# Histogram windows of a two-layer GNN in parts of 32 destinations, one exponential per attention tile, digits added by TensorE

## Chip, cores and metric

The kernel runs on one core of one Trainium2 chip. The metric is the device time of one execution in microseconds. Before the change the median of three runs was 514.59 us (514.49 to 516.25).

## What is computed

The input is a graph of 1250 nodes with 128 features and 20000 edges, sorted by destination. A first layer is a graph attention layer followed by a GRU cell, a second one is four steps of typed message passing, each followed by a GRU cell. Cut to the part that matters here:

```python
dst = minimum((1250 * uniform(20000) ** 2.0).astype(int32), 39999)   # then sorted, src with it
e = leaky_relu(s_s[src] + s_d[dst] + a_b[0], 0.2)
m = segment_max(e, dst)
ex = exp(e - m[dst])
attn = ex / segment_sum(ex, dst)[dst]
h_prime = segment_sum(attn[:, None] * Wh[src], dst) + h @ res_W.T + res_b
x = x + gru(h_prime, h)                       # layer 1
etypes = argmax(edge_feat, axis=1)
msg = (einsum('nd,tod->tno', h, W_edge) + b_edge[:, None, :])[etypes, src]
h = gru(segment_sum(msg, dst), h)             # layer 2, four times
```

## The kernel before

The kernel never gathers along edges. It first builds a table of counts: how many edges of each of four types run from a source to a destination. An edge type is worth 1, 16, 256 or 4096, so that the four counts of a cell are the four hexadecimal digits of one number below 65536. Sources stand on the 128 partitions and in 10 tiles; destinations stand along the free dimension. Attention and message passing then are dense matrix products with these counts.

The edges stand in tiles of 128, one edge on each partition. There are 157 tiles; the arrays have room for ETP = 162. The destinations are cut into NW = 20 windows of WIN = 64, and since the edges are sorted, a window touches only a few edge tiles, one after the other. For each edge tile of a window VectorE writes a one-hot of CELLS = 640 cells (10 source tiles times 64 destinations), scaled by the edge type's digit (`one_hots`, L817, into `cell_hot`), and TensorE multiplies the one-hot of the source's lane (`lane_hot`, made once, L791) with it, in two matmuls of 320 columns for the two halves of the source tiles (`window`, L1266), which add up in two PSUM banks. Both run this as a loop whose start and length are read from a table at run time (`edge_tiles`, L265: a load of the table's word into a register, and register arithmetic). A pass of the loop takes GROUP = 6 edge tiles, so a window's number of tiles is rounded up to a multiple of 6. The ring between the two engines has six one-hots: VectorE waits for `K.slot`, TensorE for `K.pair`, two tiles at a time. The table itself is computed on VectorE at the start (L714 to L781).

The order of all engines is written out by hand in a `turn(J)` for each of the 10 destination tiles of 128, that is, for windows 2J and 2J+1. On VectorE `turn(J)` (whose calls stand in the listing) is: one-hots of window 2J; `read_digits(J-1)`, which splits the 16-bit sums into low and high nibbles (L826, L827) and adds the two halves to the sums of digit pairs (L832); `weigh(J-2)`, which takes the larger of two exponentials (L856) and multiplies it with the counts (L859); the two table words of the next windows; one-hots of window 2J+1; `row_max(J-1)`, the masked maximum over sources (L839) and the small operations that make the shift of the exponentials (L843 to L851); `reciprocals(J-3)`.

On TensorE the turn is window 2J, `count_turn(J-1)` (L1284: 20 matmuls of 128 columns with fp8 weights turn the digit pairs' sums and add the two of them in PSUM), `aggregate(J-3)` (L1301), window 2J+1, `prob_turn(J-2)` (L1293). On ScalarE it is `evac` of window 2J-1 (L434), `probs_out(J-3)` (L467), `attn_out(J-4)` (L471), the two `exponentials(J-2)` (L460 for slope 1, L461 for slope 0.2), `evac` of window 2J, then `absences(J-1)` (L442), `counts_out(J-1)` (L447) and `excesses(J-1)` (L453). The leaky relu is taken inside the exponential: the larger of exp(x + a) and exp(0.2 x + b) is exp of the leaky relu.

After turn 9 the last destination tiles run through the same functions, mixed with the first layer's GRU cells (`first_front`, `first_back`) and the second layer's preparation. The four message steps follow (L1411, L1399). Counts with a digit over 15 would take a slow path in loops, which this input does not take.

## Time and profile before

| | |
|---|---|
| median of 3 runs | 514.59 us |
| the profiled execution, its own time | 513.93 us |
| its span in the trace | 512.0 us |
| mean granted TensorE clock | 0.964 |
| TensorE matmuls busy | 430.7 us (84%) |
| VectorE busy | 298.1 us (58%) |
| ScalarE busy | 186.3 us (36%) |
| one-hots L817 (VectorE), 210 instructions | 77.3 us |
| window matmuls L1266 (TensorE), 420 | 72.0 us |
| message matmuls L1411 (TensorE), 1600 | 177.1 us |

The page's busy time of an engine counts overlapping instructions once. The execution's own time lies 1.93 us above the span; the median of the runs 0.66 us above that execution's.

### The profile page before, as it was taken

Reading aid. Unit: us, or ns where it says so; the run is one execution under the profiler, and the core shown is the slowest. Engines: PE = TensorE matmul, PEld = TensorE weight load, DVE = VectorE, ACT = ScalarE, POOL = GpSimd, SP = SyncE. Lnnn points to the kernel's source line nnn. Section 1 sums busy time; section 2 is a strip of 40 time slices with the busy share of each in tenths; the row PEclk is TensorE's granted clock in tenths of the full one; section 3 lists DMA queues with packets and bytes.
Section 4 is the critical chain, followed back from the end, with each engine's and each line's share of the span. In section 5 each row is a group of like instructions: output and inputs, shape, how many; then the busy total and the mean of one; then the engine's idle time right before and its main releaser. Section 6 shows DMA issues by size and latency. Waiting matters only on the chain.

```text
span 512.0 us, 8911 instructions
## 1 busy us (share of the span) xinstructions
PE 430.7 (84%) x3132; PEld 355.0 (69%) x3132; DVE 298.1 (58%) x707; ACT 186.3 (36%) x319; POOL 12.9 (3%) x33
## 2 busy tenths in 40 slices
PE   1489766777777794687978999999999999999995
PEld 0376555556666683565657789887898878988894
DVE  6988889799999985536532454324543245433232
ACT  2631174555877786424322222122221222212111
POOL 2101000000000000100100000000000000000000
PEclk9879989899999999789998999999999999999998
DMA  7000000000000000000000000000000000000001
GB/s 165 17 2 0 0 1 1 1 1 1 1 1 2 2 2 0 1 0 0 3 6 1 2 1 0 1 1 1 0 1 2 1 2 0 1 1 1 0 22 31
DMA packets 5834, 3.56 MB, mean 7 GB/s; under 512 B 495, under 2 KB 5632, under 8 KB 5788
## 3 DMA queue, kind: packets, MB, share of 16 engines
q1 hardware_dynamic: 4516, 2.42, 1.9%
q10 hardware_dynamic: 1272, 0.54, 0.4%
q8 instruction: 28, 0.46, 0.4%
q14 instruction: 18, 0.15, 0.1%
HBM read 2.31 MB, written 0.64 MB: 6 GB/s over the span
## 4 chain that ended last, share of the span: by engine, by line
PE 65%; DVE 18%; issue 8%; ACT 5%; DVEq 3%; DMA 0%; POOL 0%; SPq 0%; ACTq 0%; POOLq 0%
PE small L1411 34%; PE big L1399 6%; PE big L1266 6%; DVE cell_hot L817 5%; DVE exp_a L856 3%; DVE absent L839 2%; PE big L1362 1%; PE big L1364 1%; PE big L1363 1%; DVEq L265 1%; PE big L1353 1%; PE big L1354 1%; PE big L1355 1%; DVEq L817 1%; PE small L1364 1%
## 5 line engine op out<-in xcount | busy, mean ns | idle before, releaser
L1411 PE MATMUL small<-nibbles,store 128*128 128x256 fp8e4 (+1 forms) x1600 | 177.1, 271 | 4.5 <-issue 4.5
L1411 PEld LDWEIGHTS small<-nibbles,store 128*128 128x128 f16 x1600 | 156.8, 98 | 26.7 <-issue 10.2
L1266 PE MATMUL big<-cell_hot,store 128*128 128x320 bf16 x420 | 72.0, 316 | 22.3 <-DVE cell_hot L817 20.3
L817 DVE TENSOR_SCALAR cell_hot<-iota,cell_w,fields 128x640 bf16<-128x640 f16 x210 | 77.3, 445 | 14.9 <-PE big L1266 6.0
L1266 PEld LDWEIGHTS big<-cell_hot,store 128*128 x420 | 51.6, 144 | 43.3 <-issue 38.5
L1066 DVE TENSOR_SCALAR aS<-small,edge_down 128x256 f32<-128x256 f32 (+1 forms) x20 | 9.6, 478 | 96.7 <-PE small L1411 96.7
L588 ACT CAST store<-digit_words 128x512 f16<-128x512 f32 x40 | 24.6, 619 | 105.3 <-DVE digit_words L979 105.3
L979 DVE TENSOR_TENSOR digit_words<-big,edge_rows 128x512 f32<-128x512 f32 x40 | 27.2, 689 | 27.4 <-PE big L1399 27.4
L1399 PE MATMUL big<-wT,h 128*128 128x512 f32 x80 | 38.1, 597 | 2.1 <-ACT h L584 2.1
L922 DVE SCALAR_TENSOR_TENSOR cell_hot<-rz,cell_hot 128x256 f32<-128x256 f32 (+1 forms) x25 | 10.5, 419 | 36.7 <-ACT cell_hot L559 36.7
L983 DVE TENSOR_TENSOR store<-digit_words,store 128x512 f16<-128x512 f32 x40 | 27.1, 687 | 2.6 <-ACT store L588 1.3
L434 ACT CAST digit_words<-big 128x640 uint16<-128x640 f32 x20 | 13.8, 692 | 36.9 <-PE big L1272 36.8
L558 ACT ACTIVATE rz<-big,gb 128x256 f32<-128x256 f32 (+1 forms) x14 | 6.6, 469 | 55.2 <-PE big L1364 55.2
L1301 PE MATMUL small<-Wh,probT 128*128 128x129 f32 x200 | 24.4, 276 | 0.0
L1301 PEld LDWEIGHTS small<-Wh,probT 128*128 128x128 f32 x200 | 23.2, 191 | 0.5 <-issue 0.5
L1399 PEld LDWEIGHTS big<-wT,h 128*128 128x128 f32 x80 | 13.8, 190 | 12.3 <-issue 9.1
L558 ACT ACTIVATE rz<-small,gb 128x256 f32<-128x256 f32 (+1 forms) x11 | 5.2, 470 | 44.7 <-PE small L1364 44.7
L1284 PE MATMUL small<-ident,digit_words 128*128 128x128 f16 x200 | 12.9, 219 | 6.7 <-DVE digit_words L832 6.7
L442 ACT ACTIVATE absent<-small,far 128x1280 f32<-128x1280 f32 x10 | 13.3, 1328 | 11.6 <-PE small L1284 11.5
L568 ACT ACTIVATE cell_hot<-cell_hot 128x256 f32<-128x256 f32 (+1 forms) x25 | 10.3, 412 | 18.6 <-DVE cell_hot L927 18.5
L1284 PEld LDWEIGHTS small<-ident,digit_words 128*128 128x128 fp8e4 x200 | 11.2, 98 | 7.6 <-DVE digit_words L832 7.6
L856 DVE TENSOR_TENSOR exp_a<-exp_a,exp_b 128x1280 f32<-128x1280 f32 x10 | 14.9, 1486 | 2.2 <-ACT exp_b L461 2.2
(237 smaller groups left out, 544.1 us busy)
## 6 DMA issues: line engine op xcount, KB each, us to landing
xn<-in_x SPq DMA_DIRECT2D x1, 576.0 KB
out<-xn SPq DMA_DIRECT2D x4, 128.0 KB
store<-in_edge_attr SPq DMA_DIRECT2D x1, 256.0 KB
wn<-in_L_gnn_W_edge SPq DMA_DIRECT2D x1, 256.0 KB, 6.6
wn<-in_L_gnn_Wi ACTq DMA_DIRECT2D x1, 192.0 KB, 4.0
wn<-in_L_gnn_Wh_g ACTq DMA_DIRECT2D x1, 192.0 KB, 6.5
wn<-in_L_gnn_W_ih SPq DMA_DIRECT2D x1, 192.0 KB, 6.3
wn<-in_L_gnn_W_hh SPq DMA_DIRECT2D x1, 192.0 KB, 6.3
```

What stands on the lines that cost most here:

```text
L434: a.copy(o.rearrange("p (b i) d -> p b i d", b=2), big[:, 2 * half:2 * half + 2, 0:HALF].rearrange("p b (i d) -> p b i d", d=WIN)).then_in ...
L442: a.activation(absent[:], smallf[:, 0:NP], ACT.Relu, bias=far[:, 0:1], scale=-FAR).then_inc(K.absent, 1)
L588: a.copy(m16[s % 2][:, i, 0], full[:, i % 2]).then_inc(T.hi, 1)
L817: last = v.tensor_scalar(cell_hot[:, slot], iota[:], cell_w[:, half, bass.ds(tile + slot, 1)], fields[:, 1, bass.ds(tile + slot, 1)], ALU. ...
L856: v.tensor_tensor(exp_a[:], exp_a[:], exp_b[:], ALU.max).then_inc(K.larger, 1)
L979: v.tensor_tensor(full[:, i % 2], big[:, i % 2], edge_rows[:], ALU.add).then_inc(T.full, 1)
L983: v.tensor_tensor(m16[s % 2][:, i, 1], full[:, i % 2], m16[s % 2][:, i, 0], ALU.subtract).then_inc(T.lo, 1)
L1266: last = mm(big[:, 2 * half + b, 0:HALF], lane_hot[:, :, bass.ds(tile + slot, 1)].rearrange("p l a -> p (l a)"), cell_hot[:, slot, b * HAL ...
L1284: last = mm(smallf[:, i * P:(i + 1) * P], pair_f8[:, i, :, b], ident16[:], start=(b == 0), stop=(b == 1), skip_group_check=True)
L1301: last = mm(psD[:, 0:P + 1], probT[:, i * P:(i + 1) * P], Wh[:, i], start=(i == 0), stop=(i == NT - 1), skip_group_check=True)
L1399: mm(big[:, i % 2], h1[:, i * P:(i + 1) * P], wT[:, W_EDGE:NWT].rearrange("p t o -> p (t o)"), start=True, stop=True).then_inc(T.ps, 1)
L1411: last = mm((psA, psD)[g % 2][:, 0:w], m16[s % 2][:, i, part, t * P:(t + 1) * P], A8[:, t % 2, i, c * CH:c * CH + w, t // 2], start=(i == ...
```

## The change

Three things are changed.

Parts of 32. A window is now handled as two parts of SUB = 32 destinations. A part has its own run of edge tiles; the table's word holds two starts and one length, the larger of the two parts' lengths, rounded up to GROUP = 4. A one-hot has 320 cells (10 source tiles times 32 destinations), and one matmul of 320 columns takes it. A pass of the loop makes four tiles of the first part and four of the second. The ring has eight half-width one-hots (RING). The zeroing matmuls before a window (L1255) have 2 columns in place of 320. The setup's tables of ranks have 40 columns in place of 20, and the table takes ten small VectorE operations in place of seven.

One exponential. `bent` is the larger of (masked + 0.8 s_dst) and 0.2 s_rows, one more VectorE pass over 1280 elements, placed in `row_max` right behind the maximum; the exponential is then taken once. `weigh` becomes one pass that limits the exponential to 1e30 and multiplies with the count. Once, at the end of turn 0, VectorE makes `s_lift` (10 elements) and `s_low` (a minimum over 1280), and ScalarE `s_flat` (1280).

Digits by TensorE. L832 goes. `count_turn` reads the nibbles directly: 40 matmuls of 128 columns in place of 20, four in each PSUM group in place of two.

```diff
-GROUP = 6
-LANE_PART = 18
+GROUP = 4
+RING = 2 * GROUP
+LANE_PART = 20
+SUB = WIN // 2
+NS = NP // SUB
...
-        cell_hot = sb("cell_hot", [P, GROUP, CELLS], BF16)
+        cell_hot = sb("cell_hot", [P, 6, CELLS], BF16)
+        half_hot = cell_hot[:].rearrange("p u c -> p (u c)")[:, 0:RING * HALF].rearrange("p (u c) -> p u c", u=RING)
...
+        bent = absent
+        s_flat = exp_b
...
-            word = eng.value_load(table[0:1, j:j + 1], min_val=0, max_val=256 * (ETP + 1))
-            first, tiles = eng.snap(word & 255), eng.snap(word >> 8)
-            return (first, tiles, ahead), eng.snap(ahead + tiles)
+            word = eng.value_load(table[0:1, j:j + 1], min_val=0, max_val=65536 * (ETP + 1))
+            first, second, tiles = eng.snap(word & 255), eng.snap((word >> 8) & 255), eng.snap(word >> 16)
+            return (first, second, tiles, ahead), eng.snap(ahead + 2 * tiles)
...
             def exponentials(n):
+                act.wait_ge(K.bent, n + 1)
                 act.wait_ge(K.shift, n + 1)
...
-                a.activation(exp_a[:], masked[:], ACT.Exp, bias=shift_col[:, 0:1])
-                a.activation(exp_b[:], masked[:], ACT.Exp, bias=shift_col[:, 1:2], scale=SLOPE).then_inc(K.exps, 1)
+                a.activation(exp_a[:], bent[:], ACT.Exp, bias=shift_col[:, 0:1]).then_inc(K.exps, 1)
...
             def one_hots(j, half, tiles_of):
-                first, tiles, ahead = tiles_of
+                first, second, tiles, ahead = tiles_of
                 dve.wait_ge(K.cellw, j + 1)
                 dve.sem_inc(K.taken, 1)
                 with dve.Fori(0, tiles, GROUP) as k:
-                    before = dve.snap(ahead + k)
-                    for u in range(0, GROUP, 2):
-                        dve.wait_ge(K.slot, before + u + 2)
-                        for slot in (u, u + 1):
-                            last = v.tensor_scalar(cell_hot[:, slot], iota[:],
-                                                   cell_w[:, half, bass.ds(tile + slot, 1)],
-                                                   fields[:, 1, bass.ds(tile + slot, 1)],
-                                                   ALU.is_equal, ALU.mult)
-                        last.then_inc(K.pair, 2)
+                    before = dve.snap(ahead + 2 * k)
+                    for b, begin in enumerate((first, second)):
+                        tile = sub_tile(begin, k)
+                        for u in range(0, GROUP, 2):
+                            dve.wait_ge(K.slot, before + b * GROUP + u + 2)
+                            for q in (u, u + 1):
+                                last = v.tensor_scalar(half_hot[:, b * GROUP + q], iota[:, b * HALF:(b + 1) * HALF],
+                                                       cell_w[:, half, bass.ds(tile + q, 1)],
+                                                       fields[:, 1, bass.ds(tile + q, 1)],
+                                                       ALU.is_equal, ALU.mult)
+                            last.then_inc(K.pair, 2)
...
             def read_digits(n):
-                v.tensor_tensor(pair_sum.rearrange("p (i d) -> p i d", i=NT), nibbles[:, 0, :, n * P:(n + 1) * P],
-                                nibbles[:, 1, :, n * P:(n + 1) * P], ALU.add).then_inc(K.conv, 1)
...
             def row_max(n, J):
+                v.scalar_tensor_tensor(bent[:], masked[:], s_lift[:, bass.ds(J, 1)], s_flat[:], ALU.add,
+                                       ALU.max).then_inc(K.bent, 1)
+                v.scalar_tensor_tensor(logit_col[:], top_col[:], s_low[:, 0:1], sd, ALU.max, ALU.add).then_inc(K.logit, 1)
...
             def weigh(n):
-                v.tensor_tensor(exp_a[:], exp_a[:], exp_b[:], ALU.max).then_inc(K.larger, 1)
-                v.tensor_tensor(exp_a[:], exp_a[:], count[:], ALU.mult).then_inc(K.probs, 1)
+                v.scalar_tensor_tensor(exp_a[:], exp_a[:], CEIL, count[:], ALU.min, ALU.mult).then_inc(K.probs, 1)
...
                 if J == 0:
                     gate_biases()
+                    v.tensor_scalar(s_lift[:], s_dst[:], 1.0 - SLOPE, None, ALU.mult).then_inc(S0.s_lift, 1)
+                    v.tensor_reduce(s_low[:], s_rows[:], AX.X, ALU.min).then_inc(S0.s_lift, 1)
...
             def count_turn(n):
-                pe.wait_ge(K.conv, n + 1)
+                pe.wait_ge(K.digits, n + 1)
...
-                    for b in range(2):
-                        last = mm(smallf[:, i * P:(i + 1) * P], pair_f8[:, i, :, b], ident16[:], start=(b == 0),
-                                  stop=(b == 1), skip_group_check=True)
+                    for q in range(TYPES):
+                        last = mm(smallf[:, i * P:(i + 1) * P], A8[:, q // 2, i, n * P:(n + 1) * P, q % 2], ident16[:],
+                                  start=(q == 0), stop=(q == TYPES - 1), skip_group_check=True)
```

The built programs differ in order at three places that matter. First, VectorE inside one pass of the one-hot loop (`cell_hot` is the ring, `iota`, `cell_w` and `fields` its inputs; REGISTER_ALU and ISA rows are register instructions of the engine's own queue). Before, the last two of six:

```order
L815 REGISTER_ALU
L817 ISA [waits k_slot]
L817 TENSOR_SCALAR cell_hot<-iota,cell_w,fields 128x640
L817 ISA
L817 TENSOR_SCALAR cell_hot<-iota,cell_w,fields 128x640
L809 ISA
L809 COMPARE_AND_BRANCH
```

Now, where a pass goes from the first part's tiles to the second's:

```order
L837 TENSOR_SCALAR cell_hot<-iota,cell_w,fields 128x320
L835 REGISTER_ALU
L837 REGISTER_ALU [waits k_slot]
L837 REGISTER_ALU
L837 ISA
L837 TENSOR_SCALAR cell_hot<-iota,cell_w,fields 128x320
```

A one-hot is half as wide, there are eight in a pass in place of six, each still with its register instruction, and there are two more register operations in the middle of the pass.

Second, VectorE between the one-hots of window 4 and those of window 5, in turn 2. Before:

```order
L826 TENSOR_SCALAR nibbles<-digit_words 128x10x128 [waits k_evac]
L827 TENSOR_SCALAR nibbles<-digit_words 128x10x128
L832 TENSOR_TENSOR digit_words<-nibbles 128x1280 [waits k_countT,k_digits]
L767 ISA
L768 TENSOR_SCALAR cell_w<-fields 128x162 [waits k_pair]
L856 TENSOR_TENSOR exp_a<-exp_a,exp_b 128x1280 [waits k_exps]
L859 TENSOR_TENSOR exp_a<-exp_a,count 128x1280 [waits k_counted,k_larger]
L265 TENSOR_LOAD table
```

Now:

```order
L846 TENSOR_SCALAR nibbles<-digit_words 128x10x128 [waits k_evac]
L847 TENSOR_SCALAR nibbles<-digit_words 128x10x128
L783 ISA
L784 TENSOR_SCALAR cell_w<-fields 128x160 [waits k_pair]
L873 SCALAR_TENSOR_TENSOR exp_a<-exp_a,count 128x1280 [waits k_counted,k_exps]
L273 TENSOR_LOAD table
```

Two wide passes are gone there, and one comes in later in the same turn, behind the masked maximum, in front of the shift:

```order
L854 ISA absent,top_col<-s_rows,absent 128x1280 [waits k_absent]
L854 ISA top_col 128x1
L858 SCALAR_TENSOR_TENSOR absent<-absent,s_lift,exp_b 128x1280 [waits k_rowmax]
L860 SCALAR_TENSOR_TENSOR logit_col<-top_col,s_low,s_dst 128x1
L862 SCALAR_TENSOR_TENSOR lmax_col<-logit_col 128x1 [waits k_logit]
L867 SCALAR_TENSOR_TENSOR shift_col<-s_dst,lmax_col 128x1 [waits k_exps,k_lmax]
```

Third, TensorE behind window 2 in turn 1, where `count_turn` stands. Before:

```order
L1272 MATMUL big<-zero 128x2 x2
L1284 MATMUL small<-ident,digit_words 128x128 [waits s0_s_rows,k_conv]
L1284 MATMUL small<-ident,digit_words 128x128 x19
L265 TENSOR_LOAD table
```

Now:

```order
L1289 MATMUL big<-zero 128x2 x2
L1301 MATMUL small<-ident,nibbles 128x128 [waits s0_s_rows,k_digits]
L1301 MATMUL small<-ident,nibbles 128x128 x39
L273 TENSOR_LOAD table
```

The count turn starts one VectorE pass earlier and has twice the matmuls; the next window's matmuls stand behind it.

## Rows read from the trace of the kernel before

**Rows 1.** Stretches: busy us and count per engine, then PE clock, DMA share, GB/s
```profile
33.00:56.90 23.90, 22.41 (x139) 16.27 (x137) 20.84 (x65) 5.49 (x15) 2.90 (x7) 1.00 0.00 1
89.80:109.70 19.90, 15.52 (x110) 11.61 (x108) 16.14 (x40) 11.09 (x13) 0.00 (x0) 0.91 0.00 1
109.70:126.00 16.30, 12.81 (x105) 10.95 (x106) 15.79 (x39) 8.73 (x11) 0.00 (x0) 1.00 0.00 1
151.30:163.80 12.50, 9.50 (x82) 7.88 (x82) 11.58 (x28) 9.55 (x12) 0.00 (x0) 1.00 0.01 2
280.00:400.00 120.00, 120.00 (x914) 100.75 (x912) 50.04 (x96) 26.73 (x56) 0.00 (x0) 1.00 0.00 1
```

**Rows 2.** Groups by line, 0 to 300 us: busy us, mean ns, idle before
```profile
L817 DVE TENSOR_SCALAR cell_hot<-iota,cell_w,fields 128x640 bf16<-128x640 f16 x210 | 77.3, 445 | 14.9 <-PE big L1266 6.0 <-issue 6.0 <-PEq L1339 2.0
```

**Rows 3.** Timeline of turn 8: start us, length us, instruction, idle before
```profile
163.76 2.23 DVE L817 TENSOR_SCALAR cell_hot<-iota,cell_w,fields 128x640 bf16<-128x640 f16 x6 [0.40 <-issue]
164.81 2.08 PE L1266 MATMUL big<-cell_hot,store 128*128 128x320 bf16 x12 [1.64 <-DVE cell_hot L817]
...
165.90 0.49 DVE L826 TENSOR_SCALAR nibbles<-digit_words 128x1280 uint16<-128x1280 uint16 x1
166.30 0.49 DVE L827 TENSOR_SCALAR nibbles<-digit_words 128x1280 uint16<-128x1280 uint16 x1
...
166.83 0.83 DVE L832 TENSOR_TENSOR digit_words<-nibbles 128x1280 uint16<-128x1280 uint16 x1
...
167.57 0.24 DVE L768 TENSOR_SCALAR cell_w<-fields 128x162 f32<-128x162 f32 x1
167.72 1.29 PE L1284 MATMUL small<-ident,digit_words 128*128 128x128 f16 x20 [0.80 <-DVE digit_words L832]
167.73 1.49 DVE L856 TENSOR_TENSOR exp_a<-exp_a,exp_b 128x1280 f32<-128x1280 f32 x1
168.84 2.45 PE L1301 MATMUL small<-Wh,probT 128*128 128x129 f32 x20
169.04 1.33 ACT L442 ACTIVATE absent<-small,far 128x1280 f32<-128x1280 f32 x1 [1.38 <-PE small L1284]
169.25 1.49 DVE L859 TENSOR_TENSOR exp_a<-exp_a,count 128x1280 f32<-128x1280 f32 x1
...
173.18 1.49 DVE L839 CUSTOM_DVE_ANT_0 absent<-s_rows,absent 128x1280 f32<-128x1280 f32 x1
...
176.21 1.16 DVE L817 TENSOR_SCALAR cell_hot<-iota,cell_w,fields 128x640 bf16<-128x640 f16 x3 [0.39 <-issue]
```

**Rows 4.** One-hot instructions and their register instructions (DVEq), durations min/median/max
```profile
L817 DVEq FUSED_REGOPS  x210: 69/93/118, 32.8 to 184.0; - x105
L817 DVE TENSOR_SCALAR cell_hot<-iota,cell_w,fields x210: 436/444/459, 32.9 to 184.7; 128x640 bf16<-128x640 f16 x105
```

**Rows 5.** Chain of waits at a window's first one-hots: start us, us, what
```profile
158.77 0.04 DVEq L815
...
159.17 0.04 DVEq L815
```

**Rows 6.** Two VectorE lines that read 256 fp32 from PSUM; durations min/median/max
```profile
L953 DVE TENSOR_TENSOR wn<-xn,big x2: 420/421/422, 209.2 to 217.3; 128x256 f32<-128x256 f32 x2
...
L927 DVE SCALAR_TENSOR_TENSOR cell_hot<-big,gb,cell_hot x14: 453/484/484, 198.4 to 506.4; 128x256 f32<-128x256 f32 x12, 128x226 f32<-128x226 f32 x2
```

**Rows 7.** Timeline, VectorE one-hots that waited for TensorE, turns 2 and 3
```profile
75.40 2.35 DVE L817 TENSOR_SCALAR cell_hot<-iota,cell_w,fields 128x640 bf16<-128x640 f16 x6 [1.16 <-PE big L1266]
...
94.16 0.80 DVE L817 TENSOR_SCALAR cell_hot<-iota,cell_w,fields 128x640 bf16<-128x640 f16 x2 [2.09 <-PE big L1266]
```

**Rows 8.** Timeline of the tail behind turn 9
```profile
191.32 1.49 DVE L856 TENSOR_TENSOR exp_a<-exp_a,exp_b 128x1280 f32<-128x1280 f32 x1 [2.17 <-ACT exp_b L461]
...
194.38 1.24 ACT L447 ACTIVATE count<-small 128x1280 f32<-128x1280 f32 x1 [1.30 <-DVE exp_a L859]
...
210.55 1.49 DVE L856 TENSOR_TENSOR exp_a<-exp_a,exp_b 128x1280 f32<-128x1280 f32 x1
```

152 lines of the change are left out of this document (79 added, 73 removed).

## The prediction

> **What bounds the kernel now.** I read the stretches first, then the groups by line, then one turn of the timeline, then the chain of waits. From 280 us on TensorE is busy all the time (120.00 of 120.00) [rows 1]; the change touches nothing there, so that part stays as it is. The histogram and attention turns, from 33 to 187 us, are another matter: in turn 8 VectorE is busy 11.58 of 12.50 us, TensorE 9.50, ScalarE 9.55; in turn 4, whose windows have twice the tiles, 15.79 of 16.30 [rows 1]. Turn 8 runs from 163.76 to 176.21, 12.45 us; within it VectorE goes from one instruction to the next, with 0.40 and some 0.3 us of its own queue's work in between, and TensorE and ScalarE wait for it (the window's matmuls 1.64 us, the count turn 0.80 us) [rows 3]. So VectorE sets the turn, and a microsecond taken from it is worth one until another loop takes over. The one-hots are the largest piece: 210 of them, 77.3 us [rows 2]. Two turns have waits of another kind: VectorE finds its ring full and waits 1.16 and 2.09 us for TensorE [rows 7].
>
> **How many one-hots there will be.** With dst = 1250 u², the edges below node d number about 20000 √(d/1250). From the drawn input, the 20 windows touch 36, 16, 12, 11, 9, 9, 8, 7, 7, 7, then 3 to 6 edge tiles; rounded up to 6 that is 36, 18, eight times 12, ten times 6 = 210, the count in [rows 2]. The larger part of each window touches 26, 9, 7, 6, 5, 5, 5, then at most 4; rounded up to 4: 28, 12, five times 8, thirteen times 4 = 132, and with two parts 264 half-width one-hots. So the work is cut by more than a third in columns (210 x 640 to 264 x 320), but the instructions rise from 210 to 264. In the last ten windows six wide ones become eight narrow ones.
>
> **What a half-width one-hot costs.** This is the number that decides. A wide one takes 0.444 us alone [rows 4], and six take 2.23, so they start (2.23 - 0.44)/5 = 0.357 us apart [rows 3]. How much of it is columns? A nibble pass of 1280 16-bit elements takes 0.49 us [rows 3]. A one-hot reads two scalars from memory; one such scalar costs 0.484 - 0.421 = 0.063 us [rows 6]. Without them a one-hot of 640 would take 0.444 - 0.126 = 0.318; 640 elements more cost 0.49 - 0.318 = 0.172. Halving a one-hot then takes off 0.086 and leaves 0.27 us from one to the next. Bounds: the 162-element pass takes 0.24 [rows 3]; if that is all fixed cost, 0.204 us belong to 478 elements, halving takes off 0.137 and leaves 0.22. At the other end width costs nothing and it stays at 0.357. I take 0.277, the first reading with 0.005 for the queue. That queue is close behind: one register instruction per one-hot, median 93 ns [rows 4], and 0.40 us from one pair's register step to the next where nothing holds it [rows 5], so 0.20 us a one-hot, before the loop's turn and the two extra register steps in mid-pass. A row that shows the queue's whole pass does not exist.
>
> The Trainium skill (VectorE: DVE Perf Modes, on the TRN2 errata) speaks against this edit: SBUF-source instructions pay a fixed latency each, which tiles of at least 512 elements are to spread, and here 640 become 320. Its figure for the cost, 58 cycles at 0.96 GHz plus the elements over the mode's factor, gives an estimate of 0.227 us for 640 elements at factor 4 and 0.144 for 320, so 47.7 to 38.0 us and a gain of 9.7. The trace does not agree with its size: it has 0.357 for the wide one.
>
> **The sum, turns 0 to 9** (against the execution's own 513.93 us; minus is time saved):
> 1. One-hots: 210 x 0.357 = 75.0 to 264 x 0.277 = 73.1: -1.9. Between its bounds: 264 x 0.22 = 58.1, -16.9; 264 x 0.357 = 94.2, +19.2.
> 2. The ring's two waits [rows 7]: -3.3. Both come where TensorE starts a window late and has two matmuls per tile to catch up; now the ring holds one whole pass of one-hots, and TensorE needs one matmul for each. If they stay, 0.
> 3. L832 is gone: it holds VectorE from 166.83 to 167.57, 0.74 us [rows 3], in turns 1 to 8: -5.9.
> 4. L856 is gone: 169.25 - 167.73 = 1.52 us [rows 3], in turns 2 to 8: -10.6. Its partner L859 becomes one combined pass of the same width, at the same 1.49.
> 5. `bent` is new: a pass over 1280 fp32 elements with one scalar from memory, like L856's 1.49 less the overlap of some 0.08, plus 0.063: 1.47, in turns 1 to 8: +11.8. Bounds 1.4 and 1.6 a pass.
> 6. `s_low`, a reduction over 1280, and the small `s_lift`: +1.6 once. By its width it is nearest to the 1.49 passes. `s_flat` on ScalarE is hidden, since ScalarE is idle most of turn 0 (busy 5.49 of 23.90) [rows 1].
> 7. Setup: ranks twice as wide, three small operations more: +0.2, with VectorE's later start hidden behind the projections on TensorE.
> Sum: -8.1. The second exponential is no term here: ScalarE has 2.95 us to spare in a turn [rows 1], and VectorE finds the exponentials ready.
>
> Turn 9 is not counted for 3 and 4, since TensorE's own row (count, aggregate, window, probabilities) already leads there.
>
> **The tail, 187 to 235 us.** Here the chain goes through the exponentials: VectorE waited 2.17 us for the second one and then made two passes before ScalarE could go on at 194.38 [rows 8]. For destination tile 8 the second exponential and L856 (1.5) go, but ScalarE now waits for the longer count turn: 20 matmuls took 1.12 us until the next (167.72 to 168.84) [rows 3], so 40 take 2.24, +1.1. I take -1.0 there. For tile 9 `bent` comes in and the exponential goes, about even, and L856 at 210.55 [rows 8] gives 1.5 more, part of it lost again to TensorE: -1.2. Tail -2.2; bounds -4.3 (everything removed counts, the count turn hidden) and +1.2.
>
> Together -8.1 - 2.2 = -10.3: 503.6 for an execution like the profiled one. The median of the runs lies 0.66 above it, so **I forecast 504 us.** The steady turn should go from 12.45 to 12.45 - 0.74 - 1.52 + 1.47 + (8 x 0.277 - 6 x 0.357 = 0.07, twice) = 11.8 us.
>
> **What is late next.** In a steady turn two loops come near. First the count: digits ready, then 2.24 + 0.17 us of matmuls, 1.33 of L442 [rows 3]: about 3.9 us until the masked maximum can start. VectorE gets there, by the present row, 173.18 - 166.79 = 6.4 us after the nibbles, less 0.74 and 1.52: 4.1 us. That leaves 0.2. Second TensorE: two windows of some 2.2, count 2.24, aggregate 2.3 (20 matmuls, 2.45 with their tail) [rows 3], probabilities 1.2: 10.2 of 11.8 us.
>
> **Rivals.**
> - *Cheaper narrow one-hots.* If a one-hot falls to 0.22 us, the sum has 15 us more, but in turns 4 to 8 the count loop allows only 0.2 to 0.3 us of it: about 11 us more, 493 us. For it: the two scalars may be less than 0.063 each here. Against: 0.22 takes the queue to its limit too. The skill's errata figure (same page and section) points this way, with 9.7 us.
> - *The count turn becomes the wait.* Every row on that path was short of slack by only 0.2 us. If 40 matmuls in groups of four take 0.5 us longer than twice 20, or TensorE starts them late, `row_max` waits 0.5 to 1 us in turns 4 to 8, and the ring's waits come back: 504 + 4 = 508. For it: TensorE's queue has more register work per matmul too.
> - *Slower: width costs nothing.* If an instruction with two scalars and a register step costs 0.357 whatever its width, then 264 x 0.08 = 21.1 us come on top: 525. The point from which it decides: at 0.32 a one-hot all the gain is used up. For it: the register instruction per one-hot. Against: the queue's pair goes in 0.40, and 162 elements take 0.24.
> - *Slower clock.* The granted clock is 1.00 in turn 8 and 0.91 in turn 3 [rows 1]; the window matmuls will leave TensorE idle more often. At 1.2 GHz a count turn doubles to 4.5 us, row_max is 2.1 us late in five turns: +10, 514.
> - *The change does not do what it says.* The guard rounds to pairs of equal length, so a window with one long part makes empty tiles; that is counted above (264), and the input fixes it. I give it nothing of its own.
>
> **Chances.** Forecast 0.50, cheaper one-hots 0.14, count wait 0.23, width costs nothing 0.08, clock 0.05. A measurement of this kernel can tell about 0.5%, 2.6 us, from no change. Faster by more than that (below 512.0): 0.50 + 0.14 + 0.21 = 0.85; the same 0.07 (a part of the count wait and of the clock case); slower 0.08. The range that holds 8 in 10 runs from the cheaper case to beyond the count wait: 492 to 510.
>
> **What would show it.** Right: 264 one-hots of 320 starting 0.27 to 0.29 us apart; a steady turn of 11.7 to 11.9; VectorE without waits for TensorE in turns 2 and 3; exponentials 10 in place of 20. Wrong: one-hots at 0.22 or over 0.32 apart; the maximum idle before it with TensorE or L442 as releaser; a turn over 12.2; a stretch of turns with the clock near 0.5.

## The result, and the profile after

| | before | after |
|---|---|---|
| median of 4 runs each, on one chip | 514.97 us (514.49 to 516.25) | 506.65 us (506.07 to 509.79) |
| the profiled execution, its own time | 513.93 us | 507.11 us |
| its span | 512.0 us | 505.3 us |
| mean granted TensorE clock | 0.964 | 0.943 |
| VectorE busy | 298.1 us | 289.9 us |
| ScalarE busy | 186.3 us | 174.2 us |
| TensorE matmuls busy | 430.7 us | 428.2 us |

The ratio of the medians is 0.9847, interval 0.9802 to 0.9892: faster by 1.5%. The forecast of 504 is 2.7 us low, and 506.65 lies in its range. What follows is about the terms under that number, several of which were not where the forecast had them.

The first thing to see is where the 6.7 us between the two spans lie. Three marks in the two timelines cut it: VectorE's first one-hot of turn 9 (176.21 in [rows 3]; 175.10 after), the first message matmul, and the last one. The group of the message matmuls gives the last two (columns: count, minimum, median and maximum ns, first and last start), of before and then of after:

```profile
L1411 PEld LDWEIGHTS small<-nibbles,store x1600: 97/98/152, 241.3 to 502.5; 128*128 128x128 f16 x178
```

```profile
L1428 PEld LDWEIGHTS small<-nibbles,store x1600: 96/98/99, 238.5 to 495.6; 128*128 128x128 f16 x178
```

| stretch | before | after | difference | forecast |
|---|---|---|---|---|
| to turn 9's first one-hot | 176.2 | 175.1 | -1.1 | -8.1 |
| from there to the first message matmul | 65.1 | 63.4 | -1.7 | -2.2 |
| first to last message matmul | 261.2 | 257.1 | -4.1 | 0 |

So the turns, for which the forecast had most of its gain, gave 1.1 us, and 4.1 us lie where the change touches nothing.

**The turns.** The one-hots' group and their register instructions, after (answers to [rows 4]):

```profile
L837 DVEq FUSED_REGOPS  x264: 69/93/118, 33.6 to 181.0; - x132
L837 DVE TENSOR_SCALAR cell_hot<-iota,cell_w,fields x264: 348/357/368, 33.8 to 181.6; 128x320 bf16<-128x320 f16 x132
```

Then turn 4 after, from its first one-hot at 112.83 to turn 5's at 124.44, as [rows 3] does turn 8 of before (start, length, instruction, count, idle before):

```profile
112.83 2.28 DVE L837 TENSOR_SCALAR cell_hot<-iota,cell_w,fields 128x320 bf16<-128x320 f16 x8 [0.46 <-issue]
115.02 0.49 DVE L846 TENSOR_SCALAR nibbles<-digit_words 128x1280 uint16<-128x1280 uint16 x1
...
115.97 2.24 PEld L1301 LDWEIGHTS small<-ident,nibbles 128*128 128x128 fp8e4 x40 [0.20 <-DVE nibbles L847]
118.42 1.33 ACT L455 ACTIVATE absent<-small,far 128x1280 f32<-128x1280 f32 x1 [1.72 <-PE small L1301]
...
119.78 1.49 DVE L854 CUSTOM_DVE_ANT_0 absent<-s_rows,absent 128x1280 f32<-128x1280 f32 x1
...
121.31 1.55 DVE L858 SCALAR_TENSOR_TENSOR absent<-absent,s_lift,exp_b 128x1280 f32<-128x1280 f32 x1
...
124.44 0.36 DVE L837 TENSOR_SCALAR cell_hot<-iota,cell_w,fields 128x320 bf16<-128x320 f16 x1 [0.48 <-issue]
```

Eight one-hots take 2.28 us, (2.28 - 0.36)/7 = 0.27 us apart. The turn takes 11.61 us. The masked maximum (L854) starts at 119.78 with no idle time listed before it: TensorE's 40 matmuls take 2.41 us, and the absence map (L455) ends at 119.75. VectorE was free at 119.65, so even here nothing is left of the forecast's slack. Now the same piece of turn 3:

```profile
102.91 3.88 PE L1301 MATMUL small<-ident,nibbles 128*128 128x128 f16 x40
...
106.82 1.33 ACT L455 ACTIVATE absent<-small,far 128x1280 f32<-128x1280 f32 x1 [3.04 <-PE small L1301]
...
108.18 1.49 DVE L854 CUSTOM_DVE_ANT_0 absent<-s_rows,absent 128x1280 f32<-128x1280 f32 x1 [2.40 <-ACT absent L455]
```

The 40 matmuls take 3.88 us, and VectorE is idle for 2.40 us before the maximum. The granted clock tells why. The first row of these stretches covers turns 1 to 9, the next the piece just shown, then turn 4, and the last two belong to the message steps below (busy us of PE, PEld, DVE, ACT, POOL, then the clock):

```profile
60.00:187.00 127.00, 98.00 (x826) 79.95 (x826) 107.91 (x297) 71.30 (x91) 0.20 (x1) 0.87 0.01 1
99.00:106.00 7.00, 6.13 (x44) 4.82 (x44) 6.78 (x20) 0.69 (x1) 0.00 (x0) 0.52 0.01 2
112.80:124.40 11.60, 9.70 (x94) 8.24 (x94) 10.79 (x29) 7.79 (x11) 0.00 (x0) 1.00 0.01 2
255.00:265.00 10.00, 6.63 (x47) 4.67 (x46) 3.24 (x5) 1.61 (x3) 0.00 (x0) 1.00 0.03 7
265.00:275.00 10.00, 10.00 (x70) 8.72 (x69) 3.90 (x9) 2.82 (x7) 0.00 (x0) 1.00 0.00 0
```

Around turn 3's count turn the clock was 0.52 of full speed, near the lower of its two levels (1.2 and 2.4 GHz); in turn 4 it was 1.00. Before the change 60 to 187 us had 0.97 (first row; the second is for the message steps):

```profile
60.00:187.00 127.00, 95.97 (x777) 77.91 (x777) 114.52 (x274) 82.32 (x99) 0.20 (x1) 0.97 0.01 1
265.00:275.00 10.00, 6.41 (x30) 4.75 (x31) 0.48 (x1) 0.00 (x0) 0.00 (x0) 0.66 0.02 5
```

VectorE's waits from 60 to 187 us after the change (total us, times, longest):

```profile
DVE absent L854 <- ACT absent L455: 8.6, 5, 2.4
DVE cell_hot L837 <- PE big L1284: 1.8, 3, 0.9
DVE cell_hot L837 <- DVE s_low L917: 0.7, 1, 0.7
```

Five of the turns wait 8.6 us together for the absence map; before the change no turn had such a wait ([rows 3] has L839 of turn 8 without one). Four of the five waits, 6.4 us, lie ahead of turn 9's first one-hot (in turns 3, 5, 6 and 8), and the fifth, 2.2 us, lies in turn 9. The 6.4 us are most of the 7.0 us by which the turns up to there missed the forecast. The ring's waits are 1.8 us in place of 3.7, and VectorE stood 0.7 us behind `s_low`.

**The message steps.** They have the same work in both kernels. The stretches above have a row for each kernel: from 265 to 275 us TensorE was busy 10.00 us at clock 1.00 after, 6.41 at 0.66 before. Its matmuls there, of before and then of after:

```profile
266.98 1.67 PE L1411 MATMUL small<-nibbles,store 128*128 128x256 fp8e4 x7 [2.87 <-issue]
270.26 2.08 PE L1411 MATMUL small<-nibbles,store 128*128 128x256 fp8e4 x9 [1.61 <-issue]
```

```profile
264.28 1.92 PE L1428 MATMUL small<-nibbles,store 128*128 128x256 fp8e4 x16 [2.91 <-issue]
266.03 0.60 PE L1370 MATMUL small<-h,wT 128*128 128x256 f32 x2
```

Both kernels have a stop of TensorE of 2.9 us, put down to its own issue. Before, the clock was low right after it, 7 matmuls took 1.67 us, and a second stop of 1.61 us came. After, 16 matmuls took 1.92. Whether this belongs to the kernel before or only to the execution that was profiled is a question for the experiments.

### The profile page after: what moved, and what is told of

The parts are those of the page before. It is cut to its first block, busy times and chain, and to the rows that moved or that the text cites. A ratio compares the mean times of both kernels' runs of the same rounds, so it can differ in the third digit from the quotient of the medians.

```text
span 505.3 us, 9333 instructions
## 1 busy us (share of the span) xinstructions
PE 428.2 (85%) x3176; PEld 354.5 (70%) x3176; DVE 289.9 (57%) x746; ACT 174.2 (34%) x310; POOL 12.0 (2%) x33
## 3 DMA queue, kind: packets, MB, share of 16 engines
HBM read 2.31 MB, written 0.64 MB: 6 GB/s over the span
## 4 chain that ended last, share of the span: by engine, by line
PE 69%; DVE 15%; issue 6%; ACT 6%; DVEq 3%; DMA 0%; POOL 0%; SPq 0%; ACTq 0%; POOLq 0%
PE small L1428 34%; PE big L1416 7%; PE big L1284 5%; PE small L1301 5%; DVE cell_hot L837 4%; DVE absent L858 3%; DVE absent L854 3%; ACT absent L455 2%; DVEq L837 2%; PE small L1318 1%; PE big L1379 1%; PE big L1381 1%; PE big L1380 1%; PE big L1370 1%; PE big L1371 1%
## 5 line engine op out<-in xcount | busy, mean ns | idle before, releaser
L1428 PE MATMUL small<-nibbles,store 128*128 128x256 fp8e4 (+1 forms) x1600 | 175.2, 270 | 2.9 <-issue 2.9
L1284 PE MATMUL big<-cell_hot,store 128*128 128x320 bf16 x264 | 60.9, 359 | 28.2 <-DVE cell_hot L837 20.2
L837 DVE TENSOR_SCALAR cell_hot<-iota,cell_w,fields 128x320 bf16<-128x320 f16 x264 | 75.2, 357 | 13.8 <-issue 6.6
L1284 PEld LDWEIGHTS big<-cell_hot,store 128*128 x264 | 36.1, 144 | 48.1 <-issue 42.1
L941 DVE SCALAR_TENSOR_TENSOR cell_hot<-rz,cell_hot 128x256 f32<-128x256 f32 (+1 forms) x25 | 10.5, 419 | 35.9 <-ACT cell_hot L575 35.9
L1301 PE MATMUL small<-ident,nibbles 128*128 128x128 f16 x400 | 29.6, 245 | 0.2
L1301 PEld LDWEIGHTS small<-ident,nibbles 128*128 128x128 fp8e4 x400 | 28.1, 113 | 0.6 <-DVE nibbles L847 0.4
L455 ACT ACTIVATE absent<-small,far 128x1280 f32<-128x1280 f32 x10 | 13.3, 1329 | 21.8 <-PE small L1301 21.8
L854 DVE CUSTOM_DVE_ANT_0 absent<-s_rows,absent 128x1280 f32<-128x1280 f32 x10 | 14.9, 1490 | 8.8 <-ACT absent L455 8.6
L584 ACT ACTIVATE cell_hot<-cell_hot 128x256 f32<-128x256 f32 (+1 forms) x25 | 10.3, 412 | 17.4 <-DVE cell_hot L946 17.3
```

Of the source, the lines that this page charges most:

```text
L455: a.activation(absent[:], smallf[:, 0:NP], ACT.Relu, bias=far[:, 0:1], scale=-FAR).then_inc(K.absent, 1)
L837: last = v.tensor_scalar(half_hot[:, b * GROUP + q], iota[:, b * HALF:(b + 1) * HALF], cell_w[:, half, bass.ds(tile + q, 1)], fields[:, 1, ...
L854: v.tensor_tensor_reduce(masked[:], s_rows[:], absent[:], 1.0, LOWEST, ALU.subtract, ALU.max, top_col[:, 0:1]).then_inc(K.rowmax, 1)
L1284: last = mm(big[:, 2 * half + b, 0:HALF], lane_hot[:, :, bass.ds(tile + q, 1)].rearrange("p l a -> p (l a)"), half_hot[:, b * GROUP + q], ...
L1301: last = mm(smallf[:, i * P:(i + 1) * P], A8[:, q // 2, i, n * P:(n + 1) * P, q % 2], ident16[:], start=(q == 0), stop=(q == TYPES - 1), s ...
L1428: last = mm((psA, psD)[g % 2][:, 0:w], m16[s % 2][:, i, part, t * P:(t + 1) * P], A8[:, t % 2, i, c * CH:c * CH + w, t // 2], start=(i == ...
```

## Experiments

The change has three parts, called P (parts of 32), E (one exponential) and D (digits by TensorE) below. Seven runs complete the table of their combinations, five more take single causes. T1 and T2 are the theories 1 and 2 of the expectations. The kernel before ran beside all of them, 39 times; its median was 514.4 us beside the first four, 514.2 beside the next four and 514.1 beside the last four.

| kernel | us, median | ratio to before, interval | first to last message matmul | first message matmul | clock, 60 to 187 |
|---|---|---|---|---|---|
| before | 514.1 to 514.4 | 1 | 261.2 | 241.3 | 0.97 |
| P | 510.55 | 0.9915 (0.9885 to 0.9944) | 258.8 | 240.5 | 0.78 |
| E | 509.33 | 0.9896 (0.9867 to 0.9924) | 262.1 | 237.6 | 0.93 |
| D | 505.63 | 0.9839 (0.9799 to 0.9880) | 257.2 | 236.7 | 0.97 |
| E, D | 509.78 | 0.9891 (0.9854 to 0.9929) | 258.6 | 241.1 | 0.91 |
| P, E | 503.38 | 0.9782 (0.9756 to 0.9809) | 256.9 | 235.4 | 0.83 |
| P, D | 511.08 | 0.9945 (0.9922 to 0.9968) | 258.7 | 240.1 | 0.88 |
| P, E, D | 505.58 | 0.9824 (0.9794 to 0.9855) | 258.9 | 238.8 | 0.88 |

The last three columns are of each kernel's profiled execution, the first message matmul being its first weight load, as in the two rows above. One execution can lie well off the median: those of E, of E with D and of the whole change here took 511.19, 511.32 and 509.10 us, each the slowest of six.

**The whole change again.** No edit.

> The changed kernel again, beside its parts on the same chip. Both theories: 7 to 9 us faster than before. In its first trace VectorE waited 8.6 us in five turns for the absence map L455; if that comes from TensorE's clock (theory 1), the waits fall again in those turns whose count turn L1301 takes 3.4 us or more in place of 2.4, though perhaps in others. If it comes from the doubled count turn alone (theory 2), they are there in every turn with single-pass windows.

It took 505.58 us, ratio 0.9824. VectorE again waits for the absence map, 7.9 us in four turns, but not in the same turns. Turn 4, which had no listed wait in the first profile, has one here:

```profile
115.30 4.01 PE L1301 MATMUL small<-ident,nibbles 128*128 128x128 f16 x40
...
120.71 1.49 DVE L854 CUSTOM_DVE_ANT_0 absent<-s_rows,absent 128x1280 f32<-128x1280 f32 x1 [1.73 <-ACT absent L455]
```

The two profiles of the same kernel side by side, from turn 3 on (us that the 40 matmuls took, and VectorE's wait before the maximum; turns 1 and 2 have 2.4 to 2.5 us and no wait):

| turn | first profile: matmuls, wait | second profile: matmuls, wait |
|---|---|---|
| 3 | 3.88, 2.40 | 3.58, 2.13 |
| 4 | 2.41, 0.13 | 4.01, 1.73 |
| 5 | 3.46, 1.27 | 2.41, 0.12 |
| 6 | 3.94, 1.42 | 2.41, 0 |
| 7 | 2.41, 0.12 | 2.41, 0.13 |
| 8 | 3.14, 1.31 | 3.48, 1.66 |
| 9 | 3.11, 2.17 | 3.30, 2.35 |

Every turn with a count turn of 3.1 us or more waits 1.3 us or more, and at 2.41 us the wait is at most 0.13. This is T1: the waits follow the slowed count turns, from 3.1 us on and not only from the 3.4 that T1 named. Turn 9's wait has a second part: its count turn starts 1.4 us after the nibbles are ready in both profiles (179.61 for 178.18 in the first).

The message steps took 258.9 us here and 257.1 in the first profile: behind the same stop the clock was 0.83 from 265 to 275 us here, and 1.00 there. So this piece differs between executions of one kernel. The turns do too: turn 9's first one-hot stands at 173.72 here and at 175.10 there.

**P alone.** Of the whole change, E and D are undone:

```diff
-                a.activation(exp_a[:], bent[:], ACT.Exp, bias=shift_col[:, 0:1]).then_inc(K.exps, 1)
+                a.activation(exp_a[:], masked[:], ACT.Exp, bias=shift_col[:, 0:1])
+                a.activation(exp_b[:], masked[:], ACT.Exp, bias=shift_col[:, 1:2], scale=SLOPE).then_inc(K.exps, 1)
...
-                    for q in range(TYPES):
+                    for b in range(2):
```

> Parts of 32 alone; two exponentials and L832 as before. Theory 1 (VectorE's sum): -1.9 for one-hots, -3.3 for the ring's waits, +0.2 setup: 5 us faster than before. The count turn has 20 matmuls and VectorE reaches the masked maximum 6.4 us after the nibbles, so no wait for L442 even at half clock. Rival (the smaller one-hots already cost their gain in clock): 0 to 2 us faster, with the granted clock under 0.95 and waits of VectorE for TensorE.

510.55 us, 3.8 us less than before, between T1's 5 and the rival's 0 to 2. The steady turn is 12.78 us, 0.33 more than before: eight narrow one-hots cost more than six wide ones. Turn 4 is 3.9 us shorter (12.86 for 16.73), but turn 1 starts 2.8 us later (59.66 for 56.90), and in its profile the turns together gain nothing: turn 9's first one-hot stands at 177.08, 0.9 us behind before. The ring's waits did not go, as T1 had it; they are 4.6 us in place of 3.7, the longest in turn 3:

```profile
99.73 1.18 DVE L832 TENSOR_SCALAR cell_hot<-iota,cell_w,fields 128x320 bf16<-128x320 f16 x4 [3.53 <-PE big L1280]
```

Of the 3.3 us between the two profiled executions (510.62 and 513.93), 2.5 stand in the message steps. TensorE has 264 window matmuls in place of 420, and the clock from 60 to 187 us is the lowest of all, 0.78. T1 was right in that nothing waits for the absence map.

**E alone.** The diff of the change in `exponentials`, `row_max` and `weigh`, with `s_lift`, `s_low` and `s_flat`:

```diff
+                v.scalar_tensor_tensor(bent[:], masked[:], s_lift[:, bass.ds(J, 1)], s_flat[:], ALU.add,
+                                       ALU.max).then_inc(K.bent, 1)
-                v.tensor_tensor(exp_a[:], exp_a[:], exp_b[:], ALU.max).then_inc(K.larger, 1)
```

> One exponential alone. Theory 1: in the turns bent replaces the maximum, -10.6 + 11.8 + 1.6 for the start = +2.8; the tail loses two exponentials and two passes, -3.3; together within 1 us of before. Rival (ScalarE's 1.37 us per turn counts too): 8 to 12 us faster.

509.33 us: 5.0 us gained, between T1's 1 and the rival's 8 to 12. The steady turn goes from 12.45 to 12.05; 0.31 of this is the idle time in front of the odd window's one-hots (158.59 us before), which is gone. With the costlier start, turn 9's first one-hot still comes 1.8 us later than before (178.00), where T1 had 2.8. From there to the first message matmul it is 59.7 us in place of 65.1, 5.4 less where T1 had 3.3.

**D alone.**

```diff
-                v.tensor_tensor(pair_sum.rearrange("p (i d) -> p i d", i=NT), nibbles[:, 0, :, n * P:(n + 1) * P],
-                                nibbles[:, 1, :, n * P:(n + 1) * P], ALU.add).then_inc(K.conv, 1)
-                    for b in range(2):
+                    for q in range(TYPES):
```

> Digits by TensorE alone, windows of 64 and two exponentials as before. Theory 1: -5.9 in the turns, +1.1 in the tail: 4.8 us faster; the count turn has slack (VectorE comes 5.7 us after the nibbles, the map is ready after 3.9), so no wait for L442. Rival (40 matmuls delay TensorE's windows): the ring's waits grow by 2 us or more and the time is within 2 us of before.

505.63 us, 8.7 less than before and far more than the 4.8 that T1 had. Turn 9's first one-hot comes 3.8 us earlier (172.44), and 4.5 us stand at the first message matmul; 4.0 us of the profiled difference are again the message steps (257.2 in place of 261.2). TensorE is busy 107.2 of the 127 us there, its clock stays at 0.97, and nothing waits for the absence map: VectorE has two wide passes between the nibbles and the maximum (the larger of the two exponentials, and the product with the counts) and not one, which leaves the count turn its time. The ring's waits are 4.8 us, 1.1 more than before.

**E and D.** Both diffs above.

> One exponential and digits by TensorE, windows of 64 as before. Theory 1 (VectorE's sum of a turn, cut off by the wait for the absence map): the turns 1 to 9 have -5.9 -10.6 +11.8 +1.6 = -3.1 and the tail about -4; so 7 to 9 us faster than before, no slower than the whole change, and a steady turn of 11.6 to 11.8. Theory 2 (the single gains add, 5.0 and 8.7): 13 us faster, steady turn below 11.2.

509.78 us, 4.2 more than D alone, though the intervals overlap and the six runs go from 505.2 to 511.3. T1 had the steady turn nearly right, 11.44 to 11.66 for its 11.6 to 11.8, but not the time: 4.4 us gained for its 7 to 9. Turns 3 and 4 are 18.9 and 19.7 us long, where D alone has 18.0 and 16.5: VectorE finds its ring full, 10.5 us in 12 places. The granted clock in these two turns is 0.91 and 0.83 here and 1.00 in both with D alone. What would explain it, and no run isolates, is that TensorE has two matmuls of 320 columns per tile and the longer count turn there, at the lower clock. The two longest waits:

```profile
105.76 2.23 DVE L823 TENSOR_SCALAR cell_hot<-iota,cell_w,fields 128x640 bf16<-128x640 f16 x6 [2.58 <-PE big L1271]
125.72 2.23 DVE L823 TENSOR_SCALAR cell_hot<-iota,cell_w,fields 128x640 bf16<-128x640 f16 x6 [3.05 <-PE big L1271]
```

**P and E, without D.** Of the whole change, D is undone:

```diff
+                v.tensor_tensor(pair_sum.rearrange("p (i d) -> p i d", i=NT), nibbles[:, 0, :, n * P:(n + 1) * P],
+                                nibbles[:, 1, :, n * P:(n + 1) * P], ALU.add).then_inc(K.conv, 1)
-                    for q in range(TYPES):
+                    for b in range(2):
```

> The whole change without digits by TensorE: L832 stays, 20 matmuls in the count turn. Theory 1: the map is ready later by L832's 0.74 and earlier by 1.1 of matmuls, so VectorE waits less for it; but the sum has 5.9 more. 4 to 7 us faster than before, so 2 to 4 slower than the whole change. Theory 2 (gains add, 3.8 and 5.0): 9 us faster.

503.38 us, the best of the eight and 10.8 less than before, more than either theory had. The clock from 60 to 187 us is even lower than with D, and yet VectorE waits 0.2 us for the absence map in place of 8.6:

```profile
60.00:187.00 127.00, 93.10 (x659) 75.11 (x660) 115.41 (x308) 71.73 (x92) 0.20 (x1) 0.83 0.00 1
```

At turn 9's first one-hot this kernel is no clear step ahead: it has 174.65, the whole change 175.10 and 173.72 in its two profiles. D's steady turn is 0.65 us shorter (11.61 to 12.26), which about pays for the waits up to there. The difference comes behind it: to the first message matmul it is 60.8 us here and 63.4 and 65.1 with D. The last count turn and the absence map of the whole change (first profile), then without D:

```profile
191.36 2.40 PE L1301 MATMUL small<-ident,nibbles 128*128 128x128 f16 x40
193.79 1.33 ACT L455 ACTIVATE absent<-small,far 128x1280 f32<-128x1280 f32 x1 [1.67 <-PE small L1301]
```

```profile
189.56 1.28 PE L1308 MATMUL small<-ident,digit_words 128*128 128x128 f16 x20
190.88 1.33 ACT L457 ACTIVATE absent<-small,far 128x1280 f32<-128x1280 f32 x1 [0.55 <-PE small L1308]
```

Two things are on this path. The last count turn starts 16.3 us behind turn 9's first one-hot with D and 14.9 without; turn 9's own wait for the map, 2.17 us with D and 0.18 without, lies in between. And it takes 1.1 us more: with D, ScalarE's map starts 4.5 us behind the nibbles' second pass (189.31, 193.79), without D 3.4 (187.50, 190.88).

**P and D.** As the change, with the two exponentials of before.

> The whole change without the one exponential: two exponentials, two passes in weigh. VectorE reaches the masked maximum 1.5 us later, so it should never wait for the absence map, even at half clock (theory 1): 8 to 10 us faster than before, steady turn 11.8 to 12.0, as good as the whole change or better. Theory 2 (gains add): 12.5 us faster.

511.08 us over 12 runs, 3.1 gained; the sum of P and D alone would be 12.5, and T1 had 8 to 10. T1 was right that VectorE never waits for the absence map. But it waits 5.6 us in 5 places for the second exponential. The count turns of turns 6 to 9 took 3.5 to 4.0 us here; that they push ScalarE's work back, and the exponential with it, is likely and was not isolated.

**The whole change with a busier TensorE.**

```diff
+                for r in range(6 * (half == 0)):
+                    mm(big[:, 2 * half + r % 2, 0:HALF], zero16[:, 0:P], zero16[:], start=True, stop=False,
+                       skip_group_check=True)
```

> The whole change with six more zeroing matmuls of 320 columns ahead of each even window, where TensorE waits 1.3 to 1.7 us for VectorE. Theory 1 (the count turn waits because TensorE's granted clock falls to half between idle stretches): fewer turns with a count turn of 3.4 us or more, VectorE's wait for L455 falls from 8.6 us to under 4, and the time by 2 to 4 us against the whole change. Rival (the clock is not moved by this filler, or the filler delays the windows): the same time or up to 3 us slower.

504.29 us, ratio 0.9806 (0.9767 to 0.9844). TensorE gets 60 more matmuls, and the clock from 60 to 187 us goes from 0.88 to 0.93:

```profile
60.00:187.00 127.00, 104.44 (x904) 84.27 (x904) 110.19 (x310) 72.42 (x93) 0.20 (x1) 0.93 0.01 1
```

The waits for the absence map fall from 8.6 and 7.9 us in the two profiles of the whole change to 4.6, with one count turn of 3.1 us or more in place of five and four, and the first message matmul starts at 235.6 in place of 238.5 and 238.8. This is T1's direction, and less than its size: it had waits under 4 us and 2 to 4 us of time, and the medians give 1.3, with overlapping intervals. So the time does not show that the busier TensorE helps, and the waits show it for one execution.

**One scalar in the one-hots.** The edge type's weight is replaced by 1.0; this leaves the types' digits out of the counts.

```diff
-                                                       fields[:, 1, bass.ds(tile + q, 1)],
+                                                       1.0,
```

> The whole change, with the weight by edge type in the 264 narrow one-hots replaced by the constant 1.0, so that each reads one scalar from memory and not two; this leaves the types' digits out of the counts. T1 (each scalar read from memory costs the one-hot some 0.06 us, as TENSOR_SCALAR of 436 against 459 ns in the kernel before hints at, and that adds to the spacing): the duration falls from 0.357 to about 0.295 us and the spacing of the one-hots from 0.273 to about 0.21, the steady turn from 11.6 to about 10.3. T2 (the spacing of narrow one-hots is set by the issue of an instruction with addresses from registers, or TensorE's loop): the duration falls but the spacing stays at 0.25 or above, or VectorE waits on the ring for TensorE, and the turn stays above 11.2.

```profile
L837 DVEq FUSED_REGOPS  x264: 57/57/83, 33.7 to 178.6; - x132
L837 DVE TENSOR_SCALAR cell_hot<-iota,cell_w x264: 290/298/311, 33.9 to 178.8; 128x320 bf16<-128x320 f16 x132
```

```profile
110.88 1.83 DVE L837 TENSOR_SCALAR cell_hot<-iota,cell_w 128x320 bf16<-128x320 f16 x8 [0.43 <-issue]
122.00 1.83 DVE L837 TENSOR_SCALAR cell_hot<-iota,cell_w 128x320 bf16<-128x320 f16 x8 [0.44 <-issue]
```

The duration falls from 357 to 298 ns, so a scalar from memory costs 0.059 us; the spacing falls to (1.83 - 0.30)/7 = 0.22. T1 holds for both. The time does not follow: 508.29 us in one run, with waits for the ring, the other sign that T2 named. The steady turn is 11.12 (110.88 to 122.00) and not 10.3, since cheaper one-hots only bring VectorE to its waits sooner:

```profile
DVE absent L854 <- ACT absent L455: 13.7, 6, 3.7
DVE cell_hot L837 <- PE big L1284: 6.8, 6, 1.8
```

**Half the count turn.** Two of the four digits are added, which leaves two edge types out of the counts.

```diff
-                    for q in range(TYPES):
+                    for q in range(2):
```

> The whole change, with the count turn of TensorE adding only two of the four digits: 20 matmuls as before in place of 40; this leaves two edge types out of the counts. T1 (the length of the count turn is what makes the third part of the change cost where the other two are there): the count turn falls from 2.4 to 1.2 us at the full clock, VectorE's waits for the absence map fall from 8 us to under 2, and the time comes to 500 to 503.5 us, at or under the 503.4 of the change without its third part, since the add of digits on VectorE is gone as well. T2 (the loss comes from elsewhere, the order of work or the clock of the chip): the waits or the time stay within 1.5 us of the whole change, 504 to 506.

The time, 30509 us, says nothing: the kernel compares the sum of its counts with the number of edges and goes to the slow path when they differ, which I had not thought of. Up to there it runs as the others do. The wait for the absence map in turns 1 to 9, and the first one-hot of turn 9:

```profile
DVE absent L854 <- ACT absent L455: 0.7, 1, 0.7
```

```profile
167.45 2.27 DVE L837 TENSOR_SCALAR cell_hot<-iota,cell_w,fields 128x320 bf16<-128x320 f16 x8 [0.47 <-issue]
```

The waits fall from 8.6 us in the first profile of the whole change (7.9 in the second) to 0.7, and turn 9 starts at 167.45, 7.65 us before the whole change's 175.10 and 8.8 us before 176.21. The clock from 60 to 187 us was 0.88, as high as in the whole change (0.87 and 0.88). So the length of the count turn is what costs, and with the table of the two profiles above, the low clock costs through it. The 8.8 us are also close to the forecast's -8.1: that sum held once the count turn was out of the way.

**P and E, with two waits moved.** VectorE's waits for `s_flat` and `s_low` are put at their use in turn 1.

```diff
+                dve.wait_ge(S0.s_flat, 1)
+                dve.wait_ge(S0.s_lift, 2)
                 v.scalar_tensor_tensor(bent[:], masked[:], s_lift[:, bass.ds(J, 1)], s_flat[:], ALU.add,
...
-                    dve.wait_ge(S0.s_lift, 2)
```

> Parts of 32 and one exponential without the third part of the change (503.4), with VectorE's waits for the minimum of the source scores and for the scaled copy of them moved from the end of turn 0 to their use in turn 1, where both are long done. T1: the 0.69 us in which VectorE stood before turn 1 goes, and 502.0 to 503.2 us comes out. T2 (turn 1 is bound by TensorE or ScalarE): no change, 503.0 to 504.0.

503.31 us, ratio 0.9788 (0.9764 to 0.9813): the same as 503.38, as T2 had it. The 0.7 us behind `s_low` is gone from the rows, and the first message matmul starts 0.6 us earlier, but no measurement of the time can tell that.

**P and E with a busier TensorE.** The edit of the busier TensorE, on P and E.

> Parts of 32 and one exponential without the third part of the change (503.4), with six more zeroing matmuls of 320 columns on TensorE ahead of each even window, that keep it busy. T1 (the granted clock costs only through the count turn of 40 matmuls, and here the count turn is short): the granted clock rises by 0.01 to 0.03, but the time stays within 1.2 us of 503.4, since VectorE does not wait for TensorE. T2 (the lower clock slows this kernel elsewhere as well): 499.5 to 502.

505.54 us, ratio 0.9838 (0.9815 to 0.9861), slower than P and E by 2.2. T1 had the clock right (0.932 to 0.946 over the whole span) but not the time, and T2 is refuted. The edit costs 2.2 us where VectorE does not wait for a count turn. The profiled execution is 1.2 us longer in its span, and 1.0 of it is there at turn 3's first one-hot (97.74 for 96.77), with one wait for the ring of 1.62 us in turn 2 in place of 0.72. For the rest there is no row.

## Why the forecast was right, and where it was not

- *Range and sign*: right. 506.65 is in 492 to 510, faster by more than 0.5%.
- *Term 1, the one-hots*: 264 of them, 0.273 us apart for the 0.277 taken. The way to it, a scalar at 0.063 us, was checked by the run with one scalar: 0.059. The figure of the Trainium skill (VectorE: DVE Perf Modes, on the TRN2 errata) that the forecast quotes is not borne out in its size: a narrow one-hot has 0.357 us alone and 0.273 in a row, for its 0.144. The forecast left out what the same section says under its table, that this row under-predicts a single operation and that about 150 fixed cycles were measured in place of 58. That gives an estimate of 0.24 us for 320 elements, and two scalars at 0.06 bring it to 0.36. What width costs agrees: 0.087 us between 640 and 320 (444 and 357 ns), for 0.083 estimated from the page's factor 4. Its warning against small tiles holds as well: with P alone the steady turn was 0.33 us longer, in the turns where six wide one-hots become eight narrow ones. The term had 0.14 for that.
- *Term 2, the ring's waits*: -1.9 in place of -3.3. The reason that the term gave was the ring of P, and with P alone the waits rose from 3.7 to 4.6 us; they are 1.8 with P and E. So the reason is not borne out by itself.
- *Terms 3 and 4, L832 and L856*: gone. D alone shortened the steady turn by 0.90 us, where the term had 0.74.
- *Term 5, `bent`*: 1.552 us, 1.47 until the next instruction (121.31 to 122.78), as taken.
- *Term 6*: `s_low` took 1.48 and VectorE stood 0.69 us behind it, 2.2 for 1.6.
- *Term 7, the setup*: +0.2 taken; the first one-hot starts at 33.76 and 34.19 in the two profiles, and not 32.93. D alone, with the setup of before, has 33.46, so a part of this differs between executions.
- *The steady turn*: 11.61 for 11.8, where the clock is at 1.00. The 0.31 us of idle time in front of the odd window's one-hots is gone here as it is with E alone, which no term counted.
- *The step that failed* is the one under "What is late next": the count loop was given 0.2 us of slack, and the forecast then let the five last turns run as if that slack always held. 2.41 us for 40 matmuls was right at the full clock, and there VectorE waited 0.13 us at most. But five count turns ran wholly or partly at the lower clock, at up to 3.9 us, and cost 8.6 us, one of them in turn 9. The turns up to there gave 1.1 us (2.5 in the second profile) for 8.1. This is the mechanism of the rival *slower clock*, with its "five turns" and its 2.1 us each (2.40 is the longest); it was given 0.05, and its 514 did not come. The rival *the count turn becomes the wait* named the same place with another cause.
- *Why the total came out all the same*: in part by luck. A miss of 7.0 us in the turns was made up by 4.1 us in the message steps, for which the forecast had 0. The medians do not depend on one profile: against them the change gave 8.3 and 8.8 us, of which 2.5 to 2.7 are seen ahead of the first message matmul in the two profiles of it. The length of the message steps goes with the clock behind the stop in all thirteen profiles that have this stretch: 256.9 to 257.3 us in the six where it stays at 1.00 from 265 to 275 us (the first profile of the whole change, D, P with E, and three more), 258.6 to 259.0 in the five at 0.83 or 0.84, and 261.2 and 262.1 in the two at 0.66 (before and E). There is one profile of before, so what its other executions do there is not seen. Their times give a bound: none of its 44 executions was under 512.54 us, 1.4 us below the profiled one, and the lowest of the whole change's ten was 504.60. So at most about 1.4 us of the 4.1 is the bad luck of that one execution, if the rest of it is typical. Why the kernel before keeps losing this time is open.
- *Do the three parts add?* No. Alone they gave 3.8, 5.0 and 8.7 us, together 8.8. E takes out the VectorE work that covered D's longer count turn, and with P TensorE has less to do and ran at a lower granted clock. The whole change is no faster than D alone (505.58 and 505.63). On top of P and E, D costs about 2 us (503.4 to 505.6; the intervals, 0.9756 to 0.9809 and 0.9794 to 0.9855, overlap slightly). The best kernel found is P and E, 503.3 to 503.4 us.

## What to carry to other kernels

When an edit moves work from the bounding engine to another, price the other engine's piece at both of its clocks, and ask whether what stood on the bounding engine between hand-over and use still covers it. A slack of 0.2 us is no slack, and the work that covered it may be what the same change removes. When several gains are worked out one by one, run at least the combination without each: here two of the three parts came out 2 us under all three.

## What the runs showed of the hardware

- The granted clock from 60 to 187 us was 0.97 before, 0.87 and 0.88 with the whole change, 0.83 with P and E, and 0.78 with P alone, the last three with 264 window matmuls in place of 420; 60 more matmuls of zeros brought 0.88 to 0.93. Less work on TensorE is not the whole of it: E alone takes nothing from TensorE and had 0.93, E with D gives it more and had 0.91, and D alone stayed at 0.97.
- The count turn of 40 matmuls of 128 columns took 2.41 us at the full clock and up to 4.1 at the lower one. With 20 matmuls it took 1.29 and 2.31, and there (P and E) VectorE waited 0.2 us for the absence map at a mean clock of 0.83.
- A stop of 2.7 to 3.1 us on TensorE, put down to its own issue, stands in all thirteen profiles that have the message steps. It comes ahead of the same matmul in each, the 149th from the first message matmul on, some 26 us behind it, so it goes with a place in the program. The clock behind it was full in one execution of the whole change and 0.83 in another, with 1.9 us between their message steps. What makes the stop is not shown.
- A scalar operand from memory costs a VectorE instruction 0.06 us (357 to 298 ns), and with one fewer the register instruction of its queue goes from a median of 93 to 57 ns.
